# Depthwise convolution stage: the last tap on four quarters of the array, high halves read from the fp32 input, one sum on GpSimd

## What is computed

```python
def _L1_conv_ref(x, dw_w, dw_b, ln_g, ln_b, w1, b1, grn_g, grn_b, w2, b2):
    y = lax.conv_general_dilated(x, dw_w, window_strides=(1, 1), padding=[(3, 3), (3, 3)],
                                 dimension_numbers=('NCHW', 'OIHW', 'NCHW'), feature_group_count=48)
    y = y + dw_b[None, :, None, None]
    y = jnp.transpose(y, (0, 2, 3, 1))
    mu = jnp.mean(y, axis=-1, keepdims=True)
    var = jnp.mean(jnp.square(y - mu), axis=-1, keepdims=True)
    y = (y - mu) * lax.rsqrt(var + EPS) * ln_g + ln_b
    y = jnp.einsum('nhwc,fc->nhwf', y, w1) + b1
    y = jax.nn.gelu(y, approximate=False)
    ...                                   # response normalisation over the image, w2, b2
    return x + y
```

## Time and profile before

| | us |
|---|---|
| median of 3 runs | 2929.57 |
| the profiled execution | 2942.04 |
| its span in the profile | 2940.4 |
| convolution phase, first to last matmul of the channels | 2227.7 to 2458.8 |

### The profile page before, as it was taken

The page is one execution under the profiler, slowest core; times in us unless marked ns, Lnnn a source line. Parts: engine busy times, 40 slices in busy tenths (PEclk is TensorE's granted clock), DMA queues, the critical chain, the costliest instruction groups (busy, mean ns, idle before and its releaser), DMA issues. The chain is left out here.

```text
span 2940.4 us, 81102 instructions
## 1 busy us (share of the span) xinstructions
PE 2583.5 (88%) x30330; PEld 1517.3 (52%) x30330; DVE 2032.3 (69%) x3231; ACT 1767.5 (60%) x3278; POOL 1337.5 (45%) x1333
## 2 busy tenths in 40 slices
PE   3999899898989898998989899899937996889997
PEld 2666565565656565565656556566513553333332
DVE  3767676666666675676667667667568996988984
ACT  1666565565656565565656566566657775655551
POOL 3555454454445454454545445455311333544552
PEclk9989999999899999999999999999958998889988
DMA  3111111111111111111111111111036995777774
GB/s 41 31 27 27 35 32 27 27 33 33 27 27 27 34 33 27 27 39 27 27 27 39 27 27 33 34 27 34 20 70 190 287 288 140 158 179 181 193 173 119
DMA packets 198492, 209.90 MB, mean 71 GB/s; under 512 B 159246, under 2 KB 160131, under 8 KB 198184
## 3 DMA queue, kind: packets, MB, share of 16 engines
q1 hardware_dynamic: 185896, 166.14, 24.1%
q0 software_dynamic: 12288, 39.07, 4.3%
HBM read 124.64 MB, written 80.58 MB: 70 GB/s over the span
## 5 line engine op out<-in xcount | busy, mean ns | idle before, releaser
L348 POOL TENSOR_TENSOR shift<-const_b,qmax 113x588 bf16<-113x588 bf16 x256 | 314.2, 1227 | 253.3 <-DVE qmax L536 253.3
L337 POOL TENSOR_TENSOR xm_l<-xh,xm_h 113x784 bf16<-113x784 f32 x128 | 214.6, 1676 | 463.5 <-DVE xm_h L456 463.5
L647 ACT ACTIVATE P<-ps_t 98x588 f32<-98x588 f32 x256 | 169.6, 662 | 337.9 <-PE ps_t L839 337.3
L375 POOL TENSOR_TENSOR sqb_l<-sq,sqb_h 113x392 bf16<-113x392 f32 x256 | 259.7, 1034 | 142.7 <-DVE sqb_h L439 142.7
L446 DVE TENSOR_TENSOR xh<-xc,rs 113x784 f32<-113x784 f32 x64 | 62.4, 976 | 349.1 <-ACT rs L632 349.0
L678 ACT ACTIVATE G<-ps_m 128x392 f32<-128x392 f32 x384 | 176.4, 501 | 130.9 <-PE ps_m L896 93.8
L830 PE MATMUL ps_t<-u_h,xs_h 113*98 113x147 bf16 x1024 | 222.9, 233 | 0.0
L830 PE MATMUL ps_t<-u_h,xs_l 113*98 113x147 bf16 x1024 | 222.5, 232 | 0.0
L830 PE MATMUL ps_t<-u_l,xs_h 113*98 113x147 bf16 x1024 | 222.4, 232 | 0.0
L536 DVE TENSOR_REDUCE qmax<-ps_s 113x12 f32<-113x588 f32 x256 | 196.3, 767 | 36.4 <-PE ps_s L809 33.4
L639 ACT CAST u_h<-ps_m 113x392 bf16<-113x392 f32 x384 | 177.4, 479 | 67.6 <-PE ps_m L784 66.1
(11 more groups left out here) (252 smaller groups left out, 7941.7 us busy)
## 6 DMA issues: line engine op xcount, KB each, us to landing
xin<-rows_scratch SPq DMA_DIRECT2D x96, 236.0 KB, 5.0
xin<-rows_scratch SPq DMA_DIRECT2D x96, 235.8 KB, 5.3
X<-x_windows SPq DMA_DIRECT2D x128, 147.0 KB, 2.9
x_scratch<-x SPq DMA_DIRECT2D x128, 147.0 KB, 2.8
y_scratch<-y POOLq DMA_DIRECT2D x96, 196.0 KB, 4.2
r_RS<-rs_scratch SPq DMA_DIRECT2D x128, 147.0 KB, 3.5
r_Y<-y_scratch SPq DMA_DIRECT2D x128, 147.0 KB, 3.8
r_X<-x_scratch SPq DMA_DIRECT2D x128, 147.0 KB, 4.0
```

Source lines behind the costliest of these rows:

```text
L337: nc.gpsimd.tensor_tensor(xm[a][1][:, r, :], xh[a][:], xm[a][0][:, r, :], ALU.subtract).then_inc(S["lo"][a], 1)
L348: nc.gpsimd.tensor_tensor(shift[:, j % 2], e, m, ALU.mult).then_inc(S["md"], 1)
L375: nc.gpsimd.tensor_tensor(sqb[a][1][:, cols], sq[a][:, cols], sqb[a][0][:, cols], ALU.subtract).then_inc(S["sq_lo"][a], 1)
L647: nc.scalar.activation(P[:, j % 2].rearrange("p (b n) h t -> p b (n h t)", b=2), ps_t[0:KEYS, :, 0:2 * HQ], ACT.Exp).then_inc(S["ex"], 1)
```

## The change

Three edits in the convolution phase:

1. The eighth column of `taps` is filled with the seventh tap, so that the band of the last pair holds the seventh tap in partitions 64 to 127 too. The 12 matmuls of the last pair, each over 64 rows as before, take the first half of the images (k = 0) from partitions 0 to 63 and the second half (k = 1) from partitions 64 to 127, so four matmuls in a row use the four quarters of the array.
2. `xp[0]` is gone. The high half is a view of `xin`: the upper 16 bits of each fp32 number, read as bf16 with a step of two elements (truncated, where it was rounded). ScalarE's copy goes. `low` on VectorE now subtracts that view from `xin`, both operands from the same tile, and waits for the DMA and for the convolution that used its slot. `load` of channel c now waits for the convolution of channel c-4, since the matmuls read `xin` itself.
3. `sum_sq += sq` moves from VectorE to GpSimd, behind the three stores of the same channel.

```diff
-        xp = [sb(f"xp_{p}", [128, RING, 2, images, PAD], BF16) for p in "hl"]
+        x_low = sb("x_low", [128, RING, 2, images, PAD], BF16)
+        x_high = xin[:].bitcast(BF16).rearrange("p s k (b w t) -> p s k b w t", w=PAD, t=2)[:, :, :, :, :, 1]
...
-                wait(sp, xp_low, c - RING + 1)
+                wait(sp, convolved, c - RING + 1)
...
+                wait(pool, sq_made, c + 1)
+                wait(pool, sq_added, c)
+                nc.gpsimd.tensor_tensor(sum_sq[:], sum_sq[:], sq[:, s % 2], ALU.add).then_inc(sq_added, 1)
+
+            pool.wait_ge(sums_cleared, 2)
...
-            k = 0
+            nc.vector.tensor_copy(taps[:, :, WS:TAPS], taps[:, :, WS - 1:WS]).then_inc(split_made, 1)
+            k = 1
+            dve.wait_ge(split_made, k)
...
-                wait(dve, xp_high, c + 1)
-                nc.vector.tensor_tensor(xp[1][:, s].rearrange("p k b w -> p k (b w)"), xin[:, s],
-                                        xp[0][:, s].rearrange("p k b w -> p k (b w)"), ALU.subtract).then_inc(xp_low, 1)
+                wait(dve, xin_loaded[s], 64 * (turn + 1))
+                wait(dve, convolved, c - RING + 1)
+                nc.vector.tensor_tensor(x_low[:, s].rearrange("p k b w -> p k (b w)"), xin[:, s],
+                                        x_high[:, s].rearrange("p k b w -> p k (b w)"), ALU.subtract).then_inc(xp_low, 1)
...
-                wait(dve, sq_made, c + 1)
-                wait(dve, sq_added, c)
-                nc.vector.tensor_tensor(sum_sq[:], sum_sq[:], sq[:, s % 2], ALU.add).then_inc(sq_added, 1)
...
-            def high(c, s, turn):
-                wait(act, xin_loaded[s], 64 * (turn + 1))
-                wait(act, convolved, c - RING + 1)
-                nc.scalar.copy(xp[0][:, s].rearrange("p k b w -> p k (b w)"), xin[:, s]).then_inc(xp_high, 1)
...
-                parts = ((0, 0), (0, 1), (1, 0))
-                for m in range(PAIRS):
-                    rows_ = 2 * SIDE if m < PAIRS - 1 else SIDE
+                parts = ((0, x_high), (0, x_low), (1, x_high))
+                for m in range(PAIRS - 1):
                     for n, (w, part) in enumerate(parts):
                         for k in range(2):
                             for side in range(2):
-                                ins = mm(ps[s][SIDE * side:SIDE * side + SIDE, k, 0:half * IMG],
-                                         band_now[0:rows_, s, w, m, :],
-                                         xp[part][0:rows_, s, side, half * k:half * (k + 1), 2 * m:2 * m + IMG],
-                                         start=(m == 0 and n == 0), stop=(m == PAIRS - 1 and n == 2))
+                                mm(ps[s][SIDE * side:SIDE * side + SIDE, k, 0:half * IMG], band_now[:, s, w, m, :],
+                                   part[:, s, side, half * k:half * (k + 1), 2 * m:2 * m + IMG],
+                                   start=(m == 0 and n == 0), stop=False)
+                for n, (w, part) in enumerate(parts):
+                    for k in range(2):
+                        lo, first = SIDE * k, WS - 1 - k
+                        for side in range(2):
+                            ins = mm(ps[s][SIDE * side:SIDE * side + SIDE, k, 0:half * IMG],
+                                     band_now[lo:lo + SIDE, s, w, PAIRS - 1, :],
+                                     part[lo:lo + SIDE, s, side, half * k:half * (k + 1), first:first + IMG],
+                                     start=False, stop=(n == 2))
```

More of the change, by code:

```diff
@@ L1032, in convolution_phase @@
         xin_loaded = [sem(f"xin_loaded{s}") for s in range(RING)]
-        xp_high = sem("xp_high")
         xp_low = sem("xp_low")
@@ L1129, in _, with low @@
                                         fill_view(0, f), ALU.subtract).then_inc(band_low, 1)
-            def low(c, s):
-                wait(dve, xp_high, c + 1)
-                nc.vector.tensor_tensor(xp[1][:, s].rearrange("p k b w -> p k (b w)"), xin[:, s],
-                                        xp[0][:, s].rearrange("p k b w -> p k (b w)"), ALU.subtract).then_inc(xp_low, 1)
+            def low(c, s, turn):
+                wait(dve, xin_loaded[s], 64 * (turn + 1))
+                wait(dve, convolved, c - RING + 1)
+                nc.vector.tensor_tensor(x_low[:, s].rearrange("p k b w -> p k (b w)"), xin[:, s],
+                                        x_high[:, s].rearrange("p k b w -> p k (b w)"), ALU.subtract).then_inc(xp_low, 1)
                 nc.vector.tensor_copy(band_now[:, s], band[:, :, c]).then_inc(band_copied, 1)
@@ L1142, in add @@
                 nc.vector.tensor_tensor(sum_y[:], sum_y[:], y[:, s], ALU.add).then_inc(y_added, 1)
-                wait(dve, sq_made, c + 1)
-                wait(dve, sq_added, c)
-                nc.vector.tensor_tensor(sum_sq[:], sum_sq[:], sq[:, s % 2], ALU.add).then_inc(sq_added, 1)
             dve.wait_ge(band_cleared, 2)
             dve.wait_ge(band_low, FILLS)
+            dve.wait_ge(xin_cleared, 1)
             for c in range(AHEAD):
-                low(c, c)
+                low(c, c, 0)
             dve.wait_ge(sums_cleared, 2)
@@ L1154, in step @@
                 add(c, s)
-                low(c + AHEAD, (s + AHEAD) % RING)
+                low(c + AHEAD, (s + AHEAD) % RING, turn + (s + AHEAD) // RING)
             channels(dve, step, C - RING)
@@ L1160, in _ @@
                 if c + AHEAD < C:
-                    low(c + AHEAD, (c + AHEAD) % RING)
+                    low(c + AHEAD, (c + AHEAD) % RING, (c + AHEAD) // RING)
             dve.wait_ge(y_added, C)
@@ L1192, in _ @@
                                ).then_inc(band_high, 1)
-            act.wait_ge(xin_cleared, 1)
-            for c in range(AHEAD):
-                high(c, c, 0)
             act.wait_ge(bias_made, 4)
[L1199 to L1207, removed]
+            channels(act, keep)
             nc.scalar.preload_act_table_set("natural_log_exp_and_others")
@@ L1216, in _ @@
             mm = nc.tensor.matmul
-            pe.wait_ge(split_made, 8)
+            pe.wait_ge(split_made, 9)
             for f in range(FILLS):
```

## The result

| | median us | runs |
|---|---|---|
| before | 2926.01 (2918.78 to 2940.01) | 7 |
| after | 2949.48 (2946.01 to 2961.55) | 7 |

The ratio is 1.0089, 95% interval 1.0059 to 1.0119: 26 us slower (17 to 35). The prediction was +14. The profiled execution of after took 2948.41 us with a span of 2946.7, only 6.3 more than the 2940.4 of before, so the first thing to settle is which part of the span speaks for the change. The phase of the change opens on GpSimd with the clearing of `xin`: at 2163.36 before, and after at

A forecast was written before the change was run, and what follows sets the result against it. TensorE bounded the old kernel at 4.78 us per channel; the shared VectorE-GpSimd path would bound the new at 5.13. L1166 at 249.7 instead of 235.7 gives +14.0, taps +0.1: 2944 against 2929.6, 8 in 10 within 2914 to 2974.

The forecast's parts named there:

- The path that VectorE and GpSimd share: Convolution loop: GpSimd's sum and VectorE's SBUF operations take turns, 0.14 to 0.19 us of the second hidden; 5.13 per channel.
- One sign: Convolution profile: GpSimd's sum would be seen at 3 us and more, having waited for x_low.
- 5.13 per channel in the mean: Convolution loop: x_low 2.12, sum 1.95, band copy 0.14 and sum_y 1.00 less 0.08 give 5.13 us per channel.
- GpSimd's stores: Convolution loop on GpSimd: three stores per channel take 1.69 us, otherwise hidden behind the shared path.
- Band copy of channel 3 at 12.6: Start of convolution: this copy ends 12.6 us after the first matmul, behind GpSimd's first sum, ending at 12.5.
- that of channel 47 at 238.3: End of convolution: 44 more channels at 5.13 us bring the last band copy to 238.3 after the first matmul.
- The tail: After the last band copy: GpSimd's three remaining channels of stores and sums take 11.4 us, until 249.6.
- The start: First y 6.38 us after the first matmul, 0.57 earlier than before; the new taps copy adds 0.1.
- The view costs nothing: TensorE's convolution matmuls: reading with a step of two bf16 adds nothing, judged from a row at half clock.
- Rival C: Convolution matmuls: the step halves PE's reading at full clock, 6.8 us per channel, some +95; with others 0.06.
- Rival A: Convolution loop: VectorE and GpSimd don't exclude each other; PE form 26 us less, DMA form 15 less; chance 0.22.
- Rival B: Convolution loop: a convoy through sq's two slots exposes GpSimd's stores, 6.1 us per channel, +47; chance 0.12.

The follow-up runs named there:

- experiment 1: The changed kernel with the sum of squares back on VectorE, view and quarters kept: ratio 0.9954 to the kernel before, 14 us faster.
- experiment 5: The changed kernel with GpSimd's sum cut to 8 of 896 columns, waits and order kept: one profiled run, channels 4.48 us apart.
- experiment 6: The changed kernel with GpSimd's sum cut to 8 columns and a GpSimd memset behind it: one profiled run, channels 4.58 us apart.
- experiment 7: The changed kernel with GpSimd's sum ahead of its channel's three stores: ratio 1.0091 to the kernel before, 27 us slower, channels 5.10 us apart.
- experiment 2: The kernel before with only the last tap on four quarters and the copied taps row: ratio 0.9933, 20 us faster, channels 4.23 us apart.

## Why the prediction held, and where its sizes were off

The forecast (+14; 2914 to 2974) has the sign, the mechanism and the range right; the measured +26 is 12 above it. In the profiled phase +14.0 became +22.5: the last band copy came 9.1 later than forecast, and what follows it was 0.7 shorter. By the prediction's steps:

- **The path that VectorE and GpSimd share: right.** The sum alone takes 2.09 (forecast 2.09, not a row of before but steps of 0.22 between types), it comes 1.95 after `x_low` (forecast 1.95), the copy ends 0.15 to 0.17 behind it (0.14). `sum_y` keeps its 1.00 and starts 0.08 early. A channel in which only this counts takes 5.13. The handover gives 0.14 back, as the rows had it. The about 115 ns that the prediction cites from the Trainium skill, "SBUF — State Buffer", section "A bandwidth-pool intuition that's wrong (but worth ruling out)", stand there for a DMA issued from GpSimd beside a VectorE copy, and between these operations they were not seen. Experiments 1, 5 and 6 exclude the rest: the loss goes with the reading sum, not with its waits and not with a write. One sign failed: the sum was to be seen at 3 us and more, having waited for `x_low`, but its median is 2.11. The stores bring GpSimd to the path only as `x_low` ends, which is the next point.
- **5.13 per channel in the mean: too small by 0.14.** In the steady stretch the band copies end at 2232.62 (channel 5) and 2433.05 (channel 43):

```profile
2230.44 2.18 DVE L1143 COPY band_now<-band 128x512 bf16<-128x512 bf16 x1
...
2430.88 2.17 DVE L1143 COPY band_now<-band 128x512 bf16 x1
```

200.43/38 = 5.27. The term that was mis-sized is GpSimd's stores, "whose three stores took 1.69" and which were taken as hidden: they are on a loop of their own. TensorE, faster than the path, has used up its lead, and starts each channel as the copy for it ends. From the copy that ends at 2343.59:

```profile
2343.83 0.59 PE L1226 MATMUL conv_ps<-xin,band_now 128*64 128x448 bf16 x4 [1.01 <-DVE band_now L1143]
...
2347.92 0.38 PE L1233 MATMUL conv_ps<-xin,band_now 64*64 64x448 bf16 x4
```

```profile
2348.43 1.01 ACT L1183 ACTIVATE y<-conv_ps,conv_bias 128x896 f32<-128x896 f32 x1 [3.36 <-PE conv_ps L1233]
```

```profile
2350.09 1.68 POOL L1096 DMA_DIRECT2D y_scratch<-y  x3 [1.53 <-ACT y L1183]
2351.78 2.10 POOL L1099 TENSOR_TENSOR sum_sq<-sum_sq,conv_sq 128x896 f32<-128x896 f32 x1
```

```profile
2351.68 2.37 DVE L1143 COPY band_now<-band 128x512 bf16 x1
```

Convolution until 2348.30, `y` until 2349.44, 0.65 until the stores are issued, 1.68 of stores, the sum, and the copy that stands behind the sum ends at 2354.05: 10.46 us, and that copy is the one of two channels later. Two turns of the path are 10.26. The two loops nearly tie, the later one wins, and the pitch runs through 5.13, 5.32, 5.14 and 5.49. (The next turn of this loop takes 10.62; in it `y` starts 0.16 later behind the last matmul, for no reason that the profile shows.) The 0.64 between `y` and its stores stood in the earlier trace rows (2345.60 to 2346.24) and was left out of the sum. Taking the stores off this loop gives 5.13 again (experiment 7). Over the 38 steps from channel 5 to 43 the 0.14 come to 5.5 us.

- **Band copy of channel 3 at 12.6: right; that of channel 47 at 238.3: it came at 247.4.** Beside those 5.5 there are collisions at both ends, where GpSimd isn't held back by `y`, and two sums fall into one channel:

```profile
2220.83 4.55 DVE L1141 TENSOR_TENSOR x_low<-xin 128x1888 bf16<-128x1888 f32 x1
...
2442.36 4.55 DVE L1141 TENSOR_TENSOR x_low<-xin 128x1888 bf16<-128x1888 f32 x1
...
2449.93 4.53 DVE L1141 TENSOR_TENSOR x_low<-xin 128x1888 bf16<-128x1888 f32 x1
```

Channel 4 takes 7.57 (2.44 over 5.13), channels 44 to 47 together 1.1 over: 5.5 + 2.4 + 1.1 = 9.0 of the 9.1. In these three an `x_low` of 2.12 is caught by a sum of 2.1 that starts 0.45 after it, and takes 4.55, not 4.07 (2.12 + 1.95): the sum then costs about 0.5 more, and it was `x_low`, which had started first, that was held. Before the last two GpSimd had stood 3 us between two stores for no reason that the profile shows (one copy took 0.28 then), and made up for it afterwards. While it did, PE waited 2.76 us for the copy that ends at 2449.01, and behind that wait, from 2449.4 to 2452.4, its granted clock was 0.58: for most of that time the lower level of 1.2 GHz. What that adds to the end of the last channels I haven't separated.

- **The tail: right in size by luck.** From the end of the last band copy to L1171 it took 10.7 (forecast 11.4), but not for the reason given. The forecast had GpSimd work off three channels of stores and sums behind PE. In the trace GpSimd had caught up and stood idle before the last two:

```profile
2457.11 1.68 POOL L1096 DMA_DIRECT2D y_scratch<-y  x3 [4.65 <-ACT y L1183]
```

The last `y` starts at 2459.86, 5.2 behind the copy, and its 1.01, the gap of 0.65, 1.68 of stores and a sum of 2.08 follow: 10.7. The tail is PE's last convolution and one channel of GpSimd.

- **The start.** First `y` 6.31 after the first matmul (6.38). `taps` and the start: +0.3 (forecast +0.1).
- **"The view costs nothing": wrong, and hidden.** The row on which it rested is at half clock; at full clock a pair takes 0.203 instead of 0.189. TensorE needs 4.4 per channel, not 4.21, still less than the path leaves it. Rival C had the right kind of effect at ten times its size (+95 against +9.7).
- **Rival A** (no exclusion, -15 to -26) didn't come, but experiment 2 shows what its PE form was worth: -20 measured, once the sum stays on VectorE and the dense copy stays too. Its DMA form fell: 309 GB/s at a share of 0.99 was read as a limit, and the same share carried 329.
- **Rival B** (a convoy through `sq`'s two slots, 6.1 per channel) didn't come in after: ScalarE's square waited for the sum once, 0.2 us. The channels of 7.6 above are another thing, two sums in one channel. Its chain is real all the same; experiment 6 shows it.
- **The rest of the program taken as unchanged: not borne out.** The response block was 4.3 longer in the profile of after, and it is longer in all five kernels with the sum on GpSimd (see the result). That could be the difference between +22.5 in the phase and the measured +26, but the interval of 17 to 35 holds both, and the cause stays open.

The sum of the parts, then, in us per channel of spacing: quarters -0.55 (experiment 2), view +0.20 (1 against 2), the sum on GpSimd +0.81 (after against 1): +0.46, or 22 us.

## What to carry to other kernels

Work moved from VectorE to GpSimd isn't taken off VectorE when both read SBUF: where the VectorE operations have two SBUF inputs or are fast copies, the moved 2.1 us came back as 1.9 us of waiting, for 1.0 us saved. Before such a move, count per iteration what each of the two would hold the path with, not what each engine would be busy with, and then walk the loop that the moved instruction closes, with every gap between its steps: two loops that tie cost more than either. Make the edits of a bundle separately: here one (the quarters, -20 us) was worth having, and the other two (+11 and +24 alone) hid it.

## What the hardware showed beyond expectation

- Reading the moving operand with a step of two bf16 costs 7% at full clock (0.203 for 0.189 us per pair of 448 columns), while at half clock no cost was seen.
- Four 64 by 64 quarters take 0.19 to 0.23 us per group of four matmuls of 448 columns (in after they start at 2347.50, 2347.73 and 2347.92), the time of one pair.
- A GpSimd memset of 2 us delays no VectorE operation with two inputs in SBUF (24 `sum_y` and 26 `x_low` ran beside one), but it makes a 0.28 us bf16 copy take 2.19.
- By the starts in the profile, the first is not always the one that keeps the path: three `x_low` that had started 0.45 us before a GpSimd sum were held until it was done, while the sum took its usual 2.08 to 2.11.
- A GpSimd instruction of 8 columns, which can take 0.2 us, took 1.84 while it waited out `x_low` (shortest 0.21, experiment 6).
- A DMA share of 1.00 to 1.01 was seen at 302, 312 and 329 GB/s in kernels with the same transfers: it isn't by itself the sign of a limit.
- A load of 128 partitions whose source has an outer dimension of 2 moved at 53 GB/s at a DMA share of 0.13, where loads of 64 partitions moved 242.
